# First attention: key maxima per single PSUM bank, and another order of products within each key tile

## The reference, cut to what matters

```python
q = _qdq(x) @ _qdq(wq).T + bq                      # (4, 512, 512): 16 heads of 32
kv = cond @ wkv.T + bkv                            # cond: (4, 1601, 512)
attn = softmax(einsum('bnhd,bmhd->bhnm', q, k) / sqrt(32))
o = einsum('bhnm,bmhd->bnhd', attn, v)
out = _qdq(o) @ _qdq(wp).T + bp                    # qdq: round to int8 steps by the row's maximum
```

## Time and profile before

| | |
|---|---|
| median of three runs | 2533.0 us |
| the profiled execution | 2530.99 us, its span 2529.2 us |
| granted TensorE clock, mean | 0.997 of full speed |
| PE busy | 2477.4 us, 98% of the span |
| DVE, ACT, POOL busy | 1791.0, 1212.2, 1189.8 us |
| first attention | 628 to about 1346 us |

### The profile page before, as it was taken

How to read it: one execution, slowest core, us unless ns; L and a number is a source line. 1 busy time by engine, 2 the same in 40 slices (tenths; PEclk the granted TensorE clock), 3 DMA queues, 4 the chain that set the end, 5 groups by cost and what they waited for, 6 DMA issues and landing times. The chain is left out here.

```text
span 2529.2 us, 33722 instructions
## 1 busy us (share of the span) xinstructions
PE 2477.4 (98%) x13168; PEld 1621.0 (64%) x13168; DVE 1791.0 (71%) x2456; ACT 1212.2 (48%) x1853; POOL 1189.8 (47%) x355
## 2 busy tenths in 40 slices
PE   8999999999999999999998999999999999999998
PEld 7988898988455555555545788788433333335786
DVE  4554554546777777777765667664899999999873
ACT  4222212311566666666663322232788888885110
POOL 0000000000688988888891000000699999996410
PEclk9999999999999999999999999999999999999999
DMA  8677786745888778887745654444998777776300
GB/s 308 207 262 236 259 292 242 228 152 160 180 166 172 165 171 168 170 183 170 151 111 203 230 175 168 141 147 113 247 203 171 168 161 170 159 177 195 106 34 34
DMA packets 225343, 452.27 MB, mean 179 GB/s; under 512 B 18936, under 2 KB 95256, under 8 KB 219360
## 3 DMA queue, kind: packets, MB, share of 16 engines
q1 hardware_dynamic: 218704, 402.93, 57.1%
q0 software_dynamic: 6480, 47.19, 9.6%
HBM read 260.63 MB, written 140.59 MB: 159 GB/s over the span
## 5 line engine op out<-in xcount | busy, mean ns | idle before, releaser
L1409 ACT ACTIVATE probs<-psum 128x512 f32<-128x512 f32 (+1 forms) x832 | 434.9, 601 | 298.1 <-PE psum L1250 276.3
L1434 DVE TENSOR_REDUCE win_max<-psum 128x1 f32<-128x802 f32 x480 | 455.5, 988 | 118.3 <-PE psum L1215 112.9
L2377 DVE TENSOR_SCALAR probs<-psum,bound 128x1024 f32<-128x1024 f32 (+1 forms) x416 | 498.9, 1275 | 30.5 <-POOL pooled L2409 20.7
L2352 ACT ACTIVATE probs<-probs 128x1024 f32<-128x1024 f32 (+1 forms) x416 | 437.5, 1058 | 81.5 <-DVE probs L2377 39.5
L2409 POOL TENSOR_TENSOR pooled<-pooled,probs 128x2048 f32<-128x2048 f32 x92 | 424.3, 4612 | 12.8 <-ACT probs L2352 0.2
L1559 POOL TENSOR_TENSOR pooled<-pooled,probs 128x2048 f32<-128x2048 f32 x78 | 366.3, 4696 | 33.5 <-DMA probs<-probs 27.9
L1250 PE MATMUL psum<-q_st,k_st 128*128 128x512 f32 (+1 forms) x832 | 293.5, 426 | 10.3 <-issue 5.6
L312 POOL TENSOR_TENSOR r_q<-ve_q,minus_half 128x4 f32<-128x4 f32 x8 | 9.1, 1133 | 611.3 <-DVE ve_q L256 611.3
L1215 PE MATMUL psum<-k_st,q_st 96*128 96x402 f32 x960 | 272.7, 365 | 2.5 <-DVE win_max L1434 2.2
L2320 PE MATMUL psum<-q_st,k_st 128*128 128x512 f32 (+1 forms) x832 | 250.6, 426 | 10.8 <-DVE probs L2377 9.7
L1215 PEld LDWEIGHTS psum<-k_st,q_st 96*128 96x128 f32 x960 | 167.6, 189 | 143.2 <-DVE win_max L1434 125.1
(11 more groups left out here) (278 smaller groups left out, 4372.9 us busy)
## 6 DMA issues: line engine op xcount, KB each, us to landing
k_st<-k_hi SPq DMA_DIRECT2D x64, 801.0 KB, 7.5
probs<-probs POOLq DMA_DIRECT2D x45, 1024.0 KB, 8.8
k_st<-k_lo SPq DMA_DIRECT2D x48, 801.0 KB, 10.8
k_hi<-kt_hi SPq DMA_DIRECT2D x32, 801.0 KB, 4.0
k_lo<-kt_lo SPq DMA_DIRECT2D x32, 801.0 KB, 6.0
v_rows<-v_out SPq DMA_DIRECT2D x96, 256.0 KB
v_st<-v_rows SPq DMA_DIRECT2D x24, 768.0 KB
q_st<-q_hi SPq DMA_DIRECT2D x64, 256.0 KB, 6.9
```

Of the source, the lines that this page charges most:

```text
L1409: A.activation(probs[i % NPROBS][0:rows, j, :], bank(score_banks.where["score", u, t, j])[0:rows, :], ACT.Exp, scale=1.0 / ROOT).then_inc( ...
L1434: V.tensor_reduce(win_max[:, r, j, c:c + 1], window(windows.where["max", u, i])[:, :, 0:MV], AX.XY, ALU.max).then_inc(max_done, 1)
L2352: A.activation(dst, dst, ACT.Exp, scale=1.0 / ROOT).then_inc(exp_done, 1)
L2377: V.tensor_scalar(probs[i % NPROBS][0:rows, half * W:half * W + W, :], window(("score", u, t, half))[0:rows], bound[0:rows, u // NG, t:t + 1],
```

## The change

1. A window becomes one matmul in one bank: 64 windows a unit in place of 32, six a step in steps 0 to 9 and four in step 10 (`WINDOWS` = 6). Banks 2, 3, 4 and 5 are taken in turn. The matmuls (64 of 402 keys a unit) stay the same ones; each now has its own wait and its own signal. DVE makes 64 reductions of 401 numbers a unit in place of 32 of 802, and `win_max` has four columns for each query and head in place of two. The stage before keeps its 32 pairs for unit 0 and uses two of the four columns.
2. `turn`, `closing`, and the first rows of the next stage take single banks; `closing` transposes the denominators first and then the accumulator, with a signal after each.
3. The order within each step is another. With M one matmul for the maxima, D the denominators:

| step | before (W: the two matmuls of a window; S: a score; V: the values) | after |
|---|---|---|
| 0, 2 to 4, 6 to 9 | S S W S W V W S | S M M V S M S M M S M |
| 1 | S W S W S S W V | M S M S V M M S S M M |
| 5 | S W D W S S W V S | M S M S S M V D M M S M |
| 10 | S W S S W S V | M S M S M S M S V |
| 11 | S V S S turn S | V S S S turn S |
| 12 | S closing S S S V | V S S S closing S |

4. ACT copies the accumulator (`copy_acc`) in step 1 ahead of the third exponential, in place of behind the fourth; `three_banks` leaves bank 7 out for the fourth score of step 5 and the first three of step 6, in place of the last three and the first one.

```diff
-            NQ, NSLOT, NPROBS, LAG, TURN_AT, WINDOWS = 3, 3, 9, 2, 11, 3
+            NQ, NSLOT, NPROBS, LAG, TURN_AT, WINDOWS = 3, 3, 9, 2, 11, 6
+            NMAX = HPG * RT * len(MCH)
-                score_banks, windows = Banks((0, 1, 7)), Banks((1, 2))
-                window = lambda slot: psum[:, 2 * slot:2 * slot + 2, :]
+                score_banks, windows = Banks((0, 1, 7)), Banks((2, 3, 4, 5))
...
-                    return u == 0 or not (t == SUM_AT and j > 0 or t == SUM_AT + 1 and j == 0)
+                    return u == 0 or not (t == SUM_AT and j == 3 or t == SUM_AT + 1 and j < 3)
...
-                        for w in range(2):
-                            start = MCH[2 * c + w]
-                            m = M.matmul(window(slot)[:, w, 0:MW], q_st[s][0:96, j, r * P:(r + 1) * P],
-                                         k_st[s][0:96, j, start:start + MW], start=True, stop=True)
-                        m.then_inc(max_ps, 1)
+                        M.matmul(bank(slot)[:, 0:MW], q_st[s][0:96, j, r * P:(r + 1) * P],
+                                 k_st[s][0:96, j, MCH[c]:MCH[c] + MW], start=True, stop=True).then_inc(max_ps, 1)
                         windows.freed_by(max_done, max_window(u, i) + 1)
...
                     def closing(u):
-                        slot, free = windows.take(("close", u))
-                        M.wait_ge(*free)
                         M.wait_ge(den_copied, u + 1)
-                        for w, src in enumerate((acc_sb, den_sb)):
+                        for w, src in enumerate((den_sb, acc_sb)):
+                            slot, free = windows.take(("close", u, w))
+                            M.wait_ge(*free)
                             for r in range(RT):
...
                         elif t == SUM_AT:
                             maxima(0)
-                            if u:
-                                sums(u - 1)
+                            scores(u, t, 0)
                             maxima(1)
                             scores(u, t, 1)
                             scores(u, t, 2)
                             maxima(2)
                             values_behind()
+                            if u:
+                                sums(u - 1)
+                            maxima(3)
+                            maxima(4)
                             scores(u, t, 3)
+                            maxima(5)
...
+                            scores(u, t, 0)
+                            maxima(0)
+                            maxima(1)
+                            values_behind()
+                            scores(u, t, 1)
+                            maxima(2)
+                            scores(u, t, 2)
+                            maxima(3)
+                            maxima(4)
+                            if u and t == close_at(u):
+                                closing(u - 1)
+                            scores(u, t, 3)
+                            maxima(5)
...
                         for j in range(HPG):
+                            if u and (t, j) == (LAG - 1, 2):
+                                copy_acc(u - 1)
...
-                        V.tensor_reduce(win_max[:, r, j, c:c + 1], window(windows.where["max", u, i])[:, :, 0:MV],
-                                        AX.XY, ALU.max).then_inc(max_done, 1)
+                        V.tensor_reduce(win_max[:, r, j, c:c + 1], bank(windows.where["max", u, i])[:, 0:MV],
+                                        AX.X, ALU.max).then_inc(max_done, 1)
```

More of the change, by code:

```diff
@@ L1305, in first_codes @@
                             M.wait_ge(*free)
-                            for w in range(2):
-                                m = transposes(window(slot)[:, w, :], first.cols, 2 * half + w)
-                            m.then_inc(q_ps, 1)
-                            windows.freed_by(q_turned, half + 1)
+                            transposes(bank(2 + r), first.cols, r).then_inc(q_ps, 1)
+                            windows.freed_by(q_turned, r // 2 + 1)
                     def first_projection():
-                        for half in range(2):
-                            slot, free = windows.take(("first", half))
+                        for r in range(RT):
+                            _, free = windows.take(("first", r), among=(2 + r,))
@@ L1314, in first_projection @@
                             M.wait_ge(*free)
-                            if half == 0:
+                            if r == 0:
                                 M.wait_ge(tables, 16 * 3)
                                 M.wait_ge(q_turned, 2)
-                            for w in range(2):
-                                rows = slice((2 * half + w) * P, (2 * half + w + 1) * P)
-                                m = products(window(slot)[:, w, :], [(first.oq_t[:, k, rows], first.wt[:, k, :])
-                                                                     for k in range(KT)])
@@ L1322, in first_projection @@
-                            m.then_inc(y_ps, 1)
-                            windows.freed_by(y_done, 2 * half + 2)
+                            rows = slice(r * P, (r + 1) * P)
+                            products(bank(2 + r), [(first.oq_t[:, k, rows], first.wt[:, k, :])
+                                                   for k in range(KT)]).then_inc(y_ps, 1)
+                            windows.freed_by(y_done, r + 1)
                     for now, behind in steps():
@@ L1469, in quantise @@
                         V.wait_ge(row_max, 1)
-                        s = own.after(V.tensor_scalar(first.step[:], quantised(0)[:, 0, 0:RT], 1.0 / 127.0, 1e-8,
+                        s = own.after(V.tensor_scalar(first.step[:], both(0)[:, 0, 0:RT], 1.0 / 127.0, 1e-8,
                                                       ALU.mult, ALU.max))
@@ L1498, in first_rows @@
                         for r in range(RT):
-                            if r % 2 == 0:
-                                V.wait_ge(y_ps, r // 2 + 1)
-                            y = window(windows.where["first", r // 2])[:, r % 2, :]
+                            V.wait_ge(y_ps, r + 1)
+                            y = bank(2 + r)
                             s = own.after(V.scalar_tensor_tensor(out=y, in0=y, scalar=first.step[:, r:r + 1],
@@ L1517, in dve_program @@
                             closing(now[0] - 1)
[L1518 removed]
+                        for one in coming[5:]:
                             max_of(*one)
```

104 lines of the change are left out of this document (50 added, 54 removed).

## The result

The changed kernel takes 2507.8 us in the median of four runs (2507.36 to 2509.24), the kernel before 2532.86: a ratio of 0.9904, 95% interval 0.9891 to 0.9917, or 25 us less. The forecast was 2509. The profiled execution took 2509.24 us, 1.4 above the median, so against the profiled one of before it shows 21.75 us of the 25.

A forecast was written before the change was run, and what follows sets the result against it. TensorE's own order, its waits and changes of mode, was taken as the bound; 1.4 + 1.9 + 12 x 1.6 + 1.2 = 23.7 us saved, so 2533.0 - 23.7 = 2509 us. Own width 2502 to 2515, range 2500 to 2526.

The forecast's parts named there:

- The step of 3.24 us: Steps 0, 2 to 4, 6 to 9: TensorE's items take 3.24 us against 3.36, 0.12 us saved each.
- The narrow slack of the second window of a step: It needs the reduction of the previous step's fourth window, with some 0.01 us to spare; no loss taken, at worst 0.12.
- no weight load of a score waiting for ScalarE: Sign expected in steps 0 to 4 and 6 to 9 if the forecast holds; 163 such waits before.
- Step 1: Same items, again 3.24 us; before, values stood last and the accumulator's copy behind all exponentials; 0.2 us saved a unit.
- Step 5: Values and denominators in a row save 0.30 us and the 0.12 wait goes, less a late bank; net 0.25 a unit.
- the 0.15 us that I had charged for its third score: In step 5, late exponentials of step 4 release the third score's bank about 0.15 us after TensorE wants it.
- Steps 10 to 12: Values of steps 10 and 11 in a row save 0.32 us, close windows cost about 0.15; net 0.17 a unit.
- 571 ns long and 0.49 us apart: VectorE's reductions of 401 numbers; six make 2.9 us a step, 0.2 more than now and under 3.24, so hidden.
- The round of 42.3 us: POOL's adds and DMA waits in one unit, just fitting the forecast unit of 42.45 us, 0.15 us below.
- the second pair's landing as the risk: POOL's round becomes the bound if the second pair DMA lands later than its 12.7 us, meeting key loads in another phase.
- Rival (a): POOL's round gates: one us more makes a unit 43.1 us, 16 us saved, 2517 us; chance 0.18.
- The ends: Outside units 2 to 13: 1.4 us saved at unit 0's stall, 1.9 in unit 1, 1.2 in unit 14.

The follow-up runs named there:

- e1: Single-bank maxima in four banks, but product order, accumulator copy's place and score banks as before the change; 2527.3 us, ratio to before 0.9982.
- e4: Changed kernel with the maxima's products in three banks (2, 3, 4) in turn in place of four; 2577.8 us, ratio 1.0181.
- e9: Changed kernel with the first score of step 11 ahead of the values, so the values of steps 10 and 11 are not in a row; 2511.1 us.
- e3: Changed kernel with the denominators of step 5 two window products behind the values in place of directly behind them; 2511.7 us.
- e8: Changed kernel with the copies of the key rows issued ahead of the loads for unit 2 and not behind them; 2508.25 us.
- e10: Changed kernel with the first two of three pair additions by DMA cut to 128 of 2048 columns; 2500.6 us.
- e12: Changed kernel with key-row copies issued first, two more tiles added on GpSimd in the last unit, next stage's root ahead of the last add; 2510.4 us.
- e5: Changed kernel with a small reduction of 32 numbers on VectorE behind every second reduction of the maxima; 2510.1 us.
- e7: Changed kernel with POOL's fourth add of each unit cut to 16 of 2048 columns; 2509.3 us.
- e11: Changed kernel with key-row copies issued first and one more tile added on GpSimd in the last unit; 2507.9 us.
- e2: Windows in pairs of banks with reductions of 802 as before, but the new order as far as pairs allow; 2564.5 us, ratio 1.0127.

## Why the prediction was right, point by point

- **What bounds it.** TensorE's own order: confirmed by the runs that moved TensorE's work or waits (e1 to e4 and e9), each of which showed in its steps and in the total.
- **The step of 3.24 us.** Forecast 3.24, measured 3.22 to 3.26. The narrow slack of the second window of a step held. The sign "no weight load of a score waiting for ScalarE" did not come true as it was written. Total waits in units 2 to 13, and one such load in step 7 of unit 6:

```profile
PEld psum L1247 <- ACT probs L1420: 82.6, 102, 0.8
```

```profile
915.03 0.19 PEld L1247 LDWEIGHTS psum<-q_st,k_st 128*128 128x128 f32 x1 [0.84 <-ACT probs L1420]
```

  That is more than the 70.9 us of the earlier trace rows. But 96 of the 102 are the score right behind the values, 0.84 us each, and cost nothing: it starts 1.00 us after the values' group does (917.27 to 918.27), as the window product did in the earlier trace rows. What is gone is the wait of 0.19 us in the middle of a step. The total of such a line is no price; its place in the step is.
- **Step 1.** 0.2 us forecast, and the group of steps 0 to 2 gave 0.40 for 0.44. But its reason was wrong in part: I had put it to the place of the values and of the accumulator's copy, and e1 gets all of it (3.24 us) with both in their old place. It was the wait for a bank pair, 0.39 us ahead of one window and 0.23 ahead of the next.
- **Step 5.** 0.37 forecast for steps 4 and 5, 0.49 measured. The 0.49 is unit 6's; the mean of units 2 to 13 is 0.38. In eight units step 5 took 4.76 to 4.78, without the 0.15 us that I had charged for its third score; in the four units with a late POOL (below) it took 4.98 or 4.99.
- **Steps 10 to 12.** 0.29 with step 9, measured 0.28.
- **VectorE.** 571 ns long and 0.49 us apart forecast, 567 and 0.484 measured. The length was to be had from two other lengths of the same instruction, the distance from a row of the same instruction in a row. The page "VectorE: DVE Perf Modes" of the Trainium skill gives, in its section on the TRN2 errata, a fixed 120 cycles for a PSUM source, by which each would be 0.54 us, an estimate from the page; the length of one came out near that, 0.567, but what shows back to back is 0.484 - 0.417 = 0.07 us of fixed cost, and the measurement decides. Its advice to tile at 512 elements and more, given there for the latency of SBUF, would have spoken against a change that is worth 1%: the added 0.2 us of VectorE's time a step lay in its idle time, and the smaller piece freed banks earlier.
- **POOL.** The round of 42.3 us was forecast to fit just below the unit, with the second pair's landing as the risk. The margin was right, the place was wrong. In the changed kernel the waits of POOL in units 2 to 13 are

```profile
POOL pooled L1566 <- DMA probs<-probs: 13.5, 7, 3.3
POOL probs L1566 <- DMA probs<-probs: 9.6, 8, 2.4
```

  (total us, times, longest). The second line is new: the second add waits for the first pair's landing. That DMA is now issued 9 to 10 us into the unit in place of 10.1, and takes 10 to 12 us in ten units of twelve where it took 8.2 to 9.8. Why it takes longer is open. Its place against the loads of keys alone is not the reason: with the groups of step 5 apart (e3) it is issued 8.8 us into the unit and 4.1 us ahead of the next load of keys, as in seven units of the changed kernel. There it takes 8.7 to 11.4 us, in e3 7.6 to 9.6, and the long units are gone in e3 (all twelve take 42.63 to 42.75). The longest unit of the changed kernel, unit 10 with 43.2 us, shows what a late landing does:

```profile
1053.93 4.58 POOL L1566 TENSOR_TENSOR pooled<-pooled,probs 128x2048 f32<-128x2048 f32 x1 [3.32 <-DMA probs<-probs]
...
1068.57 0.89 POOL L1558 DMA_DIRECT2D probs<-probs  x1
...
1073.74 4.88 POOL L1566 TENSOR_TENSOR probs<-probs 128x2048 f32<-128x2048 f32 x1
1081.03 4.57 POOL L1566 TENSOR_TENSOR probs<-probs 128x2048 f32<-128x2048 f32 x1 [2.41 <-DMA probs<-probs]
```

  POOL's first add (1073.74) starts without a gap, so POOL is late; the landing that its fifth add waited 3.32 us for, in the round before, did that. Steps 4 and 5 of unit 10 pay, with 4.02 and 4.99 us: the first exponential of step 4 starts at 1074.16, 0.08 us behind the end of POOL's eighth add of the unit before (1069.18 to 1074.08). Rival (a) is real in four units of twelve and costs 1.4 us, not 8.
- **The ends.** Units 0 and 1: 1.4 + 1.9 us forecast, 46.9 to 44.5 and 46.4 to 45.5 measured: 2.4 + 0.9, the same sum. That the place in SP's queue sets the stall was wrong (e8); less moved by the pair additions shortens it (e10). So the sum was right by luck in part: one term too small, the other too large. Unit 14 and 15 to the last denominators: 1.2 us forecast, 0.7 measured. The step "from 1272.57 on POOL runs to the end of the stage" left out that TensorE's last denominators start 10.6 us behind the end of POOL's last add (1334.47 to 1345.10): POOL's last add ended 1.9 us earlier after the start of unit 14, and TensorE gained only 0.7 of it.
- **The other stages.** They moved as a whole, but the stage begins between 627.7 and 630.1 us in the profiled runs here, and what follows its last score takes 1187 to 1190 (1192 in e12): a scatter of 1 to 3 us that is not of the change, and the reason why e5, e7, e8 and e11 can't be told from the changed kernel.

## What to carry to other kernels

- Read an engine that is busy for 98% by the starts of its instructions: the sum of the items at their closest distance against the measured step gives what is to be won, here 0.12 us of 3.36 in eight steps of thirteen, and 0.2 to 0.3 for each group of column-tiled matmuls that is put next to another.
- More instructions on an engine with idle time can buy order on the engine that paces: halving the piece that a bank slot holds, with twice the slots, is what allowed an order without waits, and neither the pieces (e1) nor the order (e2) is worth much alone. Price the added instruction at its distance back to back, and check the step sum, not the total: at 0.58 us apart in place of 0.48 the gain was zero.
- A total of waits tells nothing of their price: after the change weight loads of scores waited longer for ScalarE in sum (82.6 us for 70.9), but under a group that was running anyway.
- After a gain, look at what is just below (here a DMA's landing in POOL's round): how long it takes can change by 2 to 3 us though its own work is the same, and it may come late in another place than before.

## What the runs showed of the hardware

- TensorE's granted clock fell to 0.50 (1.2 of 2.4 GHz) around short idle times: behind 2.09 us of waiting in e12 it stood at 0.50 from 1322.7 to 1332 us, and the same eight matmuls took 1.93 us in place of 1.04. Behind the stall of 5.58 us at the start of unit 1 the kernel before shows it too:

```profile
674.60:678.50 3.90, 3.88 (x15) 2.35 (x15) 1.87 (x2) 1.68 (x3) 2.69 (x1) 0.50 0.64 132
```

  So a wait can cost more than its length. In e12 what follows the stage's last score took 4.7 us more than in the changed kernel, of which 2.09 are the wait and 0.9 the eight matmuls at the lower clock. In the changed kernel the clock fell near there as well, but for 3.4 us (0.50 from 1328.6 to 1332.0).
- The accumulating DMA of 1 MB between SBUF tiles lands after 7 to 13 us, and how long each of a unit's three takes differs between kernels that issue the same ones: in units 2 to 13, before, the second took 11.7 to 13.0 us and the first 8.2 to 9.8; after, they take 9.8 to 13.4 and 8.7 to 12.3; with the groups of step 5 apart (e3), 10.2 to 11.9 and 7.6 to 9.6. The third takes 7.0 to 9.2 in all of these. What decides it stays open.
